# Wider stationary operand in the split value products of a transformer block

## The chip, the cores and the metric

The kernel is one program on one core of one Trainium2 chip. The metric is the device time of one execution in microseconds; the time before is the median of three executions. The profile is of one further execution, with its own time.

## The reference, cut to what matters

The kernel computes a conditioned transformer block on `x` of 2 x 2048 x 576 (16 heads of 36, a hidden layer of 2304):

```
q, k, v = split(modulate(rmsnorm(x)) @ qkv_w.T + qkv_b)      # q, k normed per head
attn = softmax(q @ k.T)                                      # per row of the batch and head
o = attn @ v                                                 # <- the change is in this product
x = x + gate_msa * (o @ proj_w.T + proj_b)
x = x + gate_mlp * (gelu(modulate(rmsnorm(x)) @ fc1_w.T + fc1_b) @ fc2_w.T + fc2_b)
```

All is float32. Where the kernel multiplies in the type fp32r, it splits operands into a high and a low part and adds the products of the parts.

## The kernel before

There are two phases. The first (`qkv_phase`, lines 115 to 630) computes q, k and v and writes them to scratch tensors in HBM. The second (`main_phase`, lines 649 to 1500) has an attention stage and then a stage of projection and MLP. In the trace the attention stage lies between about 480 and 1960 us.

The attention stage runs over 64 units `u`. A unit is one pair of heads, one row of the batch and one block of 512 queries. In a unit there are 16 blocks `kt` of 128 keys. For each one TensorE computes the scores of both heads transposed (`score`, line 1361: two products, each with 110 rows and 128 columns of stationary `kT` and 512 moving columns of `qT`), ScalarE takes the exponential of both heads at once (line 1017), and TensorE multiplies the exponentials with v.

This last product has two forms. For the eight key blocks 4 to 11 (`WHOLE`) it is `value` (lines 1372 and 1373): plain float32, with a stationary of 64 columns for one head and of 37 for the other. For the other eight (`SPLITS`) it is `split_value` (line 1386), which the change touches. VectorE has split the exponentials into `p_hi` (line 1187) and `p_lo` (line 1193). For each of the two heads TensorE multiplies `p_hi` and then `p_lo`, 128 x 512 each, by the same stationary `vx`. That makes 4 products for one key block, 32 in a unit, 2048 in the kernel.

`vx[r]` is a tile of 128 x 8 x 2 x 128: for each split key block and each head it has 128 columns. For head 0 these are 64 columns of the high part of v and then 64 of its low part; for head 1 it is the low part first. In each 64, the first 36 are v and the next is the column of ones that gives the sum of the exponentials. `split_v` (lines 1170 to 1180) writes all 128 of them, and the columns behind the 37th of a half come from a scratch tensor that was filled with ones. Before the change a product uses the first `VW` = 64 + 36 + 1 = 101 columns and writes rows 0 to 100 of a PSUM bank, `OA` for head 0 and `OBK` for head 1. Those who read the banks, `take_oa` on VectorE (line 1140) and `take_ob` on ScalarE (line 1023), read rows 0 to 100.

The order of TensorE's work is written out by hand (lines 1452 to 1476). A unit starts with three scores, then alternates the four split products of a key block with the two score products of another, has another run of three scores in the middle and one near the end, and ends with the eight `value` pairs. Split products of a unit's last four key blocks run in the next unit. A split group waits once, for the `p_lo` of its key block (line 1383). The projection of the first block, `proj` (line 1404: 14 products with 128 columns), is fitted between the units from `LAST` = 60 on.

Of the kernel before, what the change touches and what calls it, by code (L numbers as in the profile page):

```python
# [22 lines left out]
BLK = 512  # L23
# [12 lines left out]
VW = 64 + HD + 1  # L36
# [8 lines left out]
def wait(eng, sem, value):  # L45

    if isinstance(value, int) and value <= 0:
        return
    eng.wait_ge(sem, value)
# [599 lines left out]
def main_phase(nc, ctx, ps, qk_hi, qk_lo, v_s, m_s, l_s, oh_s, ol_s, xT, w2, wp, w1, outT, ident, ones, unbounded, mod, gate_b,  # L649
# [12 lines left out]
    def at(name, shape, dt, offset):  # L662
        return nc.alloc_sbuf_tensor_at(name, shape, dt, offset=offset)
# [18 lines left out]
    vx = [at(f"vx{j}", [P, NS, 2, VP], F32R, VX + j * 8 * NS * VP) for j in range(B)]  # L682
# [160 lines left out]
    with nc.Block() as block:  # L843
# [497 lines left out]
        def _(pe):  # L1341
# [33 lines left out]
            def split_value(u, j):  # L1375

                r, q = u // C % B, NS * u + j
                if u % C == 0 and j == 0:
                    pe.wait_ge(v_split, 4 * (u // C + 1))
                if j == 0:  # L1380
                    wait(pe, oa_evac, u)
                    wait(pe, ob_evac, u)
                pe.wait_ge(plo_done, q + 1)
                for h, out in enumerate((OA, OBK)):
                    for n, part in enumerate((p_hi[:, q % HIGHS], p_lo[:, j])):
                        mm = pe.matmul(out[0:VW], vx[r][:, j, h, 0:VW], part[:, h * BLK:(h + 1) * BLK],  # L1386
                                       start=j == 0 and n == 0, stop=j == NS - 1 and n == 1)
                mm.then_inc(rv_mm, 1)

# [62 lines left out]
            for u in range(NU):  # L1452
                for kt in range(3):
                    score(u, kt)
                for j in range(EARLY):
                    if u > 0:
                        split_value(u - 1, EARLY + j)
                    if j < 3:
                        score(u, 3 + j)
                if u in (LAST + 1, LAST + 2):  # L1460
                    proj(0, 2 * (u - LAST) - 1)
                for kt in range(6, 9):
                    score(u, kt)
                for j in range(3):
                    split_value(u, j)
                    score(u, 9 + j)
                if LAST <= u < LAST + 3:
                    if u == LAST:
                        pe.wait_ge(wplo_done, KC)
                    proj(0, 2 * (u - LAST))  # L1470
                for kt in range(12, 15):
                    score(u, kt)
                split_value(u, 3)
                score(u, 15)
                for kt in WHOLE:
                    value(u, kt)
# [75 lines left out]
```

## Time and profile before

| | us |
|---|---|
| median of 3 executions | 3021.05 |
| lowest, highest | 3019.34, 3022.63 |
| the profiled execution | 3016.58 |
| its span, first to last instruction | 3014.8 |

The granted TensorE clock over the span is 0.99 of full speed. TensorE (PE) is busy for 97% of the span, VectorE (DVE) for 66%, ScalarE (ACT) for 53%, GpSimd (POOL) for 7%. Busy times of matmuls overlap, since a matmul's record reaches into the next one: so a product's price on TensorE is read from the distance between the starts of two products, or from a piece of the chain of waits divided by its count, and not from its mean duration. PEld is the loading of stationary operands, which lies beside the matmuls.

### The profile page before, as it was taken

The page shows a single profiled execution, that of the slowest core. Times are in us where ns is not written, and L with a number is a line of the kernel's source. Part 1 is how long each engine was busy: PE and PEld are TensorE (multiplying, and loading weights), DVE is VectorE, ACT ScalarE, POOL GpSimd, SP SyncE. Part 2 cuts the span into 40 slices and gives each one's busy share as a digit, 9 for nine tenths or more (in the row PEclk, how much of TensorE's full clock was granted, in tenths as well). Part 3 has the DMA queues.
Part 4 walks back from the last instruction along what each step waited for, and adds up shares of the span by engine and source line. Part 5 has one row for each costly group of instructions (what it writes and reads, how often), then busy time and mean ns, then how long its engine had stood idle before and what let it go on. Part 6 is the DMA issues. An engine that isn't in the chain of part 4 may idle for free.

```text
span 3014.8 us, 35206 instructions
## 1 busy us (share of the span) xinstructions
PE 2920.2 (97%) x12968; PEld 2134.4 (71%) x12968; DVE 2003.6 (66%) x2687; ACT 1593.7 (53%) x1926; POOL 220.3 (7%) x153
## 2 busy tenths in 40 slices
PE   8999996999999999999999999999999999999998
PEld 7898994566566566566565566678888888888886
DVE  5887775888888888888888888744243342424332
ACT  3333324677677677677677676634343443434342
POOL 3232301000000000000000000080000000000000
PEclk9999997999999999999999999999999999999999
DMA  5464545122222222222222223242222222322121
GB/s 209 145 191 157 173 137 157 58 84 74 71 85 75 60 82 75 71 85 74 63 79 75 73 83 96 75 163 66 93 88 71 83 75 75 96 94 88 40 70 44
DMA packets 238406, 282.84 MB, mean 94 GB/s; under 512 B 34912, under 2 KB 143968, under 8 KB 237344
## 3 DMA queue, kind: packets, MB, share of 16 engines
q1 hardware_dynamic: 232992, 270.18, 28.9%
q10 hardware_dynamic: 5248, 10.49, 1.0%
q8 instruction: 99, 1.62, 0.2%
q14 instruction: 67, 0.55, 0.1%
HBM read 195.66 MB, written 84.67 MB: 93 GB/s over the span
## 4 chain that ended last, share of the span: by engine, by line
PE 78%; ACT 3%; DVE 2%; DMA 1%; SPq 0%; issue 0%; POOL 0%; DVEq 0%; POOLq 0%
PE ps L1386 16%; PE ps L1361 15%; PE ps L1445 14%; PE ps L1428 14%; PE ps L1373 13%; PE ps L1404 4%; ACT prob L1017 2%; PE ps L1372 2%; ACT gated L1070 1%; DVE x L1244 0%; DMA x<-xT 0%; DMA lt<-osb 0%; DVE w_lo L1238 0%; SPq L861 0%; DVE x L1248 0%
## 5 line engine op out<-in xcount | busy, mean ns | idle before, releaser
L1017 ACT ACTIVATE p_r<-ps 128x1024 f32<-128x1024 f32 x512 | 482.5, 1033 | 405.0 <-PE ps L1361 405.0
L1361 PE MATMUL ps<-qT,kT 110*128 110x512 f32 x2048 | 594.9, 402 | 34.1 <-DMA qT<-m_scratch 19.7
L1193 DVE TENSOR_TENSOR p_lo<-p_r,p_hi 128x1024 fp32r<-128x1024 f32 x512 | 612.8, 1217 | 0.0
L1017 ACT ACTIVATE prob<-ps 128x1024 f32<-128x1024 f32 x512 | 498.1, 1032 | 48.2 <-PE ps L1361 47.9
L1361 PEld LDWEIGHTS ps<-qT,kT 110*128 110x128 f32 x2048 | 376.8, 189 | 205.0 <-issue 51.6
L1187 DVE CAST p_hi<-p_r 128x1024 fp32r<-128x1024 f32 x512 | 353.9, 695 | 164.4 <-ACT p_r L1017 161.6
L1372 PE MATMUL ps<-prob,vp 128*64 128x512 f32 x1024 | 453.2, 595 | 0.0
L1373 PE MATMUL ps<-prob,vp 128*37 128x512 f32 x1024 | 451.8, 594 | 0.0
L1316 DVE TENSOR_TENSOR a_lo<-act,a_hi 128x512 fp32r<-128x512 f32 x144 | 102.0, 709 | 523.0 <-ACT a_hi L1060 523.0
L1445 PE MATMUL ps<-a_hi,w 128*128 128x512 f32 x1296 | 416.7, 394 | 2.9 <-DVE a_lo L1316 2.9
L1386 PE MATMUL ps<-p_hi,vx 128*101 128x512 f32 x1024 | 406.0, 397 | 0.0
L1386 PE MATMUL ps<-p_lo,vx 128*101 128x512 f32 x1024 | 403.9, 394 | 0.0
L1058 ACT ACTIVATE act<-ps,f1b_t 128x512 f32<-128x512 f32 x144 | 99.2, 689 | 511.4 <-PE ps L1428 511.4
L1373 PEld LDWEIGHTS ps<-prob,vp 128*37 128x37 f32 x1024 | 111.5, 114 | 248.3 <-issue 248.3
L1428 PE MATMUL ps<-mh_hi,w_hi 128*128 128x512 f32 x720 | 282.9, 393 | 4.1 <-DVE w_lo L1238 4.1
L1445 PEld LDWEIGHTS ps<-a_hi,w 128*128 128x128 f32 x1296 | 244.1, 188 | 56.1 <-DVE a_lo L1316 3.3
L1445 PE MATMUL ps<-a_lo,w 128*128 128x512 f32 x720 | 281.2, 391 | 0.0
L1428 PE MATMUL ps<-mh_hi,w_lo 128*128 128x512 f32 x720 | 280.5, 390 | 0.0
L1428 PE MATMUL ps<-mh_lo,w_hi 128*128 128x512 f32 x576 | 225.3, 391 | 0.0
L1386 PEld LDWEIGHTS ps<-p_lo,vx 128*101 128x101 f32 x1024 | 171.1, 167 | 68.9
L1386 PEld LDWEIGHTS ps<-p_hi,vx 128*101 128x101 f32 x1024 | 169.0, 165 | 57.6 <-issue 1.5
L593 PE MATMUL ps<-w_hi,h_hi 128*128 128x432 f32 x640 | 182.5, 366 | 9.6 <-DVE h_hi L70 8.2
(163 smaller groups left out, 3617.7 us busy)
## 6 DMA issues: line engine op xcount, KB each, us to landing
w_raw<-w SPq DMA_DIRECT2D x144, 320.0 KB, 2.9
qk_hi_scratch<-aw SPq DMA_DIRECT2D x32, 576.0 KB, 3.1
qk_lo_scratch<-aw SPq DMA_DIRECT2D x32, 576.0 KB, 4.4
kT<-qk_hi_scratch SPq DMA_DIRECT2D x128, 144.0 KB
qT<-qk_hi_scratch SPq DMA_DIRECT2D x128, 144.0 KB
v_scratch<-stv SPq DMA_DIRECT2D x32, 512.0 KB, 2.7
vp<-v_scratch SPq DMA_DIRECT2D x16, 1024.0 KB, 9.4
xb<-xT SPq DMA_DIRECT2D x8, 1280.0 KB, 10.1
```

The source lines that it names most:

```text
L593: mm = pe.matmul(ps[:, q, 0:PIECE], a[:, r, k, cols], w[:, k, q * PIECE:(q + 1) * PIECE], start=k == 0 and n == 0, stop=k == KF and n == 1)
L1017: act.activation(out, ps[:, 2 * slot:2 * slot + 2, :].rearrange("p a b -> p (a b)"), ACT.Exp).then_inc(exp_done, 1)
L1187: dve.tensor_copy(p_hi[:, q % HIGHS], p_r[:, j]).then_inc(phi_done, 1)
L1193: dve.tensor_tensor(p_lo[:, j], p_r[:, j], f32(p_hi[:, q % HIGHS]), ALU.subtract).then_inc(plo_done, 1)
L1316: dve.tensor_tensor(a_lo[:, slot], act32[:, slot], f32(a_hi[:, slot]), ALU.subtract).then_inc(alo_done, 1)
L1361: mm = pe.matmul(ps[:, 2 * (entry % RING) + h, :], kT[r][:, h, kt * P:(kt + 1) * P], qT[:, u % 2, h], start=True, stop=True)
L1372: pe.matmul(OA[0:64], vp[r][:, kt, 0:64], prob[:, j, 0:BLK], start=False, stop=False)
L1373: pe.matmul(OBK[64:VW], vp[r][:, kt, 64:VW], prob[:, j, BLK:2 * BLK], start=False, stop=False).then_inc(fv_mm, 1)
L1386: mm = pe.matmul(out[0:VW], vx[r][:, j, h, 0:VW], part[:, h * BLK:(h + 1) * BLK], start=j == 0 and n == 0, stop=j == NS - 1 and n == 1)
L1404: mm = pe.matmul(proj_bank(i, m), w[:, k, m * P:(m + 1) * P], a[:, k], start=k == 0 and n == 0, stop=k == KF and n == 1)
L1428: mm = pe.matmul(ps[:, 5 + slot, :], w[:, slot, c], a[:, i % 2, c], start=c == 0 and n == 0, stop=c == KF and n == 1)
L1445: mm = pe.matmul(ps[:, m, :], w, a[:, slot], start=k == 0 and n == 0, stop=k == FC - 1 and n == len(parts) - 1)
```

## The change

In `split_value` the product takes all 128 columns of `vx` for the key block and head, and writes all 128 rows of the bank. Nothing else differs.

```diff
                 for h, out in enumerate((OA, OBK)):
                     for n, part in enumerate((p_hi[:, q % HIGHS], p_lo[:, j])):
-                        mm = pe.matmul(out[0:VW], vx[r][:, j, h, 0:VW], part[:, h * BLK:(h + 1) * BLK],
+                        mm = pe.matmul(out, vx[r][:, j, h], part[:, h * BLK:(h + 1) * BLK],
                                        start=j == 0 and n == 0, stop=j == NS - 1 and n == 1)
                 mm.then_inc(rv_mm, 1)
```

## Rows read from the trace of the kernel before

**Rows 1.** The page: busy us, share of the span and instructions of each engine.
```profile
PE 2920.2 (97%) x12968; PEld 2134.4 (71%) x12968; DVE 2003.6 (66%) x2687; ACT 1593.7 (53%) x1926; POOL 220.3 (7%) x153
```

**Rows 2.** The page: chain that ended last, share of the span by line.
```profile
PE ps L1386 16%; PE ps L1361 15%; PE ps L1445 14%; PE ps L1428 14%; PE ps L1373 13%; PE ps L1404 4%; ACT prob L1017 2%; PE ps L1372 2%; ACT gated L1070 1%; DVE x L1244 0%; DMA x<-xT 0%; DMA lt<-osb 0%; DVE w_lo L1238 0%; SPq L861 0%; DVE x L1248 0%
```

**Rows 3.** Windows: us, busy us and count by engine, clock, DMA share, GB/s.
```profile
1400.00:1600.00 200.00, 198.12 (x853) 119.28 (x852) 172.13 (x231) 137.53 (x151) 0.00 (x0) 1.00 0.26 74
2400.00:2600.00 200.00, 199.82 (x875) 163.99 (x874) 70.25 (x98) 80.51 (x121) 0.00 (x0) 1.00 0.25 80
```

**Rows 4.** Chain in order of time, attention stage: start us, us, what, count.
```profile
1494.87 0.48 PE ps L1361 x2
...
1508.62 0.93 PE ps L1386 x4
1509.55 0.46 PE ps L1361 x2
1510.01 0.93 PE ps L1386 x4
1510.94 0.47 PE ps L1361 x2
1511.40 0.93 PE ps L1386 x4
1512.33 1.37 PE ps L1361 x6
```

**Rows 5.** Groups by form: busy us, mean ns of one, idle before.
```profile
L1386 PE MATMUL ps<-p_hi,vx 128*101 128x512 f32 x1024 | 406.0, 397 | 0.0
...
L1386 PEld LDWEIGHTS ps<-p_lo,vx 128*101 128x101 f32 x1024 | 171.1, 167 | 68.9
L1386 PEld LDWEIGHTS ps<-p_hi,vx 128*101 128x101 f32 x1024 | 169.0, 165 | 57.6 <-issue 1.5 <-DVE oa L1140 0.6
...
L1404 PEld LDWEIGHTS ps<-o_hi,wp_lo 128*128 128x128 f32 x200 | 37.6, 188 | 8.0
```

**Rows 6.** Timeline of PE from 1508.4: start us, us, instruction.
```profile
1508.46 0.40 PE L1386 MATMUL ps<-p_hi,vx 128*101 128x512 f32 x1
1508.69 0.40 PE L1386 MATMUL ps<-p_lo,vx 128*101 128x512 f32 x1
```

**Rows 7.** Timeline of PEld from 1507.5.
```profile
1508.46 0.17 PEld L1386 LDWEIGHTS ps<-p_lo,vx 128*101 128x101 f32 x1
1508.69 0.16 PEld L1386 LDWEIGHTS ps<-p_hi,vx 128*101 128x101 f32 x1
```

**Rows 8.** Chain in order of time: projection products from 1855 and from 1874.
```profile
1856.14 3.21 PE ps L1404 x14
...
1876.11 3.17 PE ps L1404 x14
```

**Rows 9.** Chain in order of time, MLP stage, from 2600.
```profile
2600.89 3.19 PE ps L1428 x14
```

**Rows 10.** Waits of VectorE: us in total, times, longest.
```profile
DVE oa L1140 <- PE ps L1386: 30.4, 59, 0.5
```

**Rows 11.** Waits of weight loads: us in total, times, longest.
```profile
PEld ps L1361 <- ACT prob L1017: 39.4, 64, 0.6
...
PEld ps L1386 <- issue: 1.5, 5, 0.4
...
PEld ps L1386 <- DVE oa L1140: 0.6, 2, 0.3
```

## The prediction

> **What bounds the kernel now.** I read the page's busy times first. TensorE is busy for 97% of the span and VectorE, the next, for 66% [rows 1]. The chain that ended last says where it counts: the split products of line 1386 are its largest single line, 16% of the span, and the scores of line 1361 have 15% [rows 2]. Then the windows, since the share of the whole span mixes stages: in the 200 us from 1400, in the attention stage, TensorE has work for 198.12 us, VectorE for 172.13 and ScalarE for 137.53 [rows 3]. So in the stage of the change TensorE sets the pace, and VectorE, which splits the exponentials, has 14% to spare. A nanosecond more or less on each split product arrives in the time nearly whole, 2048 times.
>
> What a split product costs now can't be read from its mean duration of 397 ns [rows 5], because the records overlap. In the timeline two of them start 0.23 us apart [rows 6]. The chain has the better number, pieces of 0.93 us for four: 0.93 / 4 = 232.5 ns each [rows 4]. Check: 2048 x 232.5 ns = 476 us, and 16% of 3014.8 us is 482 us [rows 2]. It holds.
>
> **The change part by part.** There is one edit, and it has four effects to price.
>
> *The stationary load.* It reads 128 columns where it read 101. The loads at line 1386 take 165 and 167 ns on average, and a load of 128 columns at line 1404 takes 188 [rows 5]: 22 ns more. Is that on the path? The load of the next product starts with the running product, at 1508.46 both, takes 0.17 us, and the next product starts at 1508.69 [rows 6, 7]. So 232.5 - 166 = some 66 ns lie between the end of a load and the start of its product. With 188 ns there remain 44. The running product's stream hides the load, and 22 of the 66 ns of cover are used up. If the cover were gone altogether, the price would be 22 ns x 2048 = 45 us. The rows of 128 columns say it is not gone: with the 188 ns load, products start 227 to 229 ns apart (next paragraph).
>
> *The distance between two products.* The moving operand is 512 columns before and after, so the stream of a product is the same. What the trace doesn't show is a split product with 128 columns, so I bound its distance by products that have them. Below: the projection in the middle of the attention stage, beside the same work of VectorE and ScalarE, 3.17 / 14 = 226.4 ns, and 3.21 / 14 = 229.3 at another place [rows 8]; the first MLP product 3.19 / 14 = 227.9 [rows 9]. Above: the scores between the split groups, which also load 128 columns (but 110 rows), 0.46 / 2 = 230 to 0.47 / 2 = 235, and once 0.48 / 2 = 240 ns [rows 4]; six scores in a row take 1.37 / 6 = 228.3. So the bounds per split product are 226.4 - 232.5 = -6.1 ns and 240 - 232.5 = +7.5 ns, which is -12.5 us and +15.4 us over 2048.
>
> I choose 230.5 ns, 2 ns less than now, or -4.1 us. The reason: long runs of one form with 128 columns go at 226 to 229 wherever they are, and no run with 101 columns does; but the scores right beside the split products have 128 columns and don't go faster than these, which says that most of the excess comes from alternating between forms, operands and banks, and that stays. The score rows are the nearest in place and pattern, so I stay nearer to them.
>
> At this place a rule can be weighed. By the Trainium skill, page "TensorE: Matmul & The Clock Gate", section "Back-to-back issue gap", the distance of products at full clock follows from the moving columns alone. With it the sum would be zero, since 512 stays 512. The trace agrees in part: the distance hardly depends on the stationary's width, but rows of one moving width range from 226.4 to 240 ns [rows 4, 8], above the page's 216, so something else adds 10 to 24 ns, and that is where this change could act.
>
> *Exposed loads.* Where the load comes after a wait, its whole length counts. At line 1386 that is so 5 + 2 times, with 1.5 and 0.6 us in total [rows 11]: 7 x 22 ns = 0.2 us, nothing. If each of the 512 split groups had its first load exposed it would be 11 us; the rows say they don't, since VectorE's parts are ready before. The 64 waits of a score's load for ScalarE (39.4 us, [rows 11]) are in the scores, and their length is set by the exponential of an earlier score; they neither shrink nor grow.
>
> *Rows 101 to 127 of the banks.* They are written and read by nobody. `take_oa` waits for the last split product (59 times, 30.4 us, [rows 10]) and reads 101 rows as before. VectorE's split of v already covers 128 columns, and no transfer changes. Cost 0; a cost would have to be in writing more rows of PSUM, and the projection's 128 rows at 226.4 ns [rows 8] show none. Nor is anything late next if the products come closer: even 12.5 us over the 64 units is 0.2 us in a unit of some 22.5, against the 14% that VectorE has free.
>
> Sum: -4.1 us + 0.2 us = -3.9 us. The profiled execution took 3016.58 us, 4.5 us less than the median of 3021.05 and 1.8 us more than its span. As nothing in the change touches what lies around the span, I put the difference on the median: 3017.1 us.
>
> **The rivals.**
>
> *The partial width is what costs.* Then all split products fall to the distance of the projection's. For it: no piece of line 1386 is under 0.93 us for four, while each long run of full-width products beside it is faster [rows 4, 8]. Against it: the scores between the split groups are full-width and at 230 to 235 ns [rows 4], and the projection at 1856 has 229.3. Time: 3021.05 - 12.5 = 3008.6 us. A rule of the skill (same page, section "Weight-path perf modes") would point this way: a fast weight load is on with exactly 128 weights of a type that is not FP32. The trace speaks against its being at work here, 188 ns for the 128-column load against 165 for 101 [rows 5], and a load that is hidden gains nothing by being faster; by it the sum would be at most this rival's.
>
> *The longer load costs* (the other side). Mechanism: the stationary for the next product is read while the moving operand streams, and has to be in place some time before the swap. The cover falls from 66 to 44 ns. If the swap needs more than 44 ns, or if the longer reading holds up the stream, each split product gets later, as the scores may be showing with 235 to 240 ns in the places where they alternate. It decides as soon as the distance passes 232.5 + 3 = 235.5 ns. At 237.5, the middle of 235 and 240, it is +5 x 2048 ns = +10.2 us: 3031.3 us. Against it: the 188 ns load under a distance of 226.4 ns [rows 5, 8] leaves only 38 ns and costs nothing.
>
> *The clock.* More columns at work could bring the granted clock down. The MLP stage, full width throughout and TensorE busy for 199.82 of 200 us, has 1.00 [rows 3], so I give it no more than a part of the slower case.
>
> **How the numbers follow.** What a measurement of this kernel can tell from no change is about 0.2%, 6 us, or 3 ns per split product. The forecast (230.5 ns, with values from 229.5 to 235.5) has 0.50 and is within it. The rival of the partial width, with gains of 3 to 6 ns, has 0.36, and the slower one 0.14. The range reaches down to 3007, the faster rival with 1.6 us of scatter (half of that of the three runs), and up to 3027, where +6 us is the end of the within case; beyond it lies most of the slower case and little of the others.
>
> **What the profile of the changed kernel would show.** The loads at line 1386 in the form 128*128 with a mean of 188 ns. The pieces of line 1386 in the chain: 0.92 for four if I am right, 0.91 or less for the first rival, 0.95 or more for the slower one. VectorE's and ScalarE's busy times and the clock of 1.00 unchanged. The scores' pieces unchanged; if they too move, the distance belongs to the pair of neighbours and not to the product, and my count of 2048 is too small. The forecast is wrong if the line's share of the chain falls by more than 6 us or grows at all beyond that.

## The result, and the profile after

The changed kernel takes 3014.16 us (median of 15 executions) against 3020.88 us for the kernel before beside it (15 executions): ratio 0.9979, 95% interval 0.9971 to 0.9986. It is faster by some 6 us, 0.2%, and the interval lies clear of no change. The forecast was 3017.1 us.

The page of the changed kernel, busy times and then the chain by line, as in [rows 1, 2]:

```profile
PE 2912.2 (97%) x12968; PEld 2178.5 (72%) x12968; DVE 2002.6 (67%) x2687; ACT 1590.7 (53%) x1926; POOL 219.1 (7%) x153
...
PE ps L1386 16%; PE ps L1361 15%; PE ps L1445 15%; PE ps L1428 14%; PE ps L1373 13%; PE ps L1404 4%; ACT prob L1017 2%; PE ps L1372 2%; ACT gated L1070 1%; DVE x L1244 0%; DMA lt<-osb 0%; DMA w_raw<-w 0%; DVE w_lo L1238 0%; DMA kT<-qk_hi_scratch 0%; DVE x L1248 0%
```

Only PEld has grown, by 44 us: 2048 loads that are 22 ns longer. The windows of the same two stages [rows 3] show the same, and the clock at 1.00; the second window, where nothing was changed, is the control:

```profile
1400.00:1600.00 200.00, 198.33 (x856) 126.46 (x856) 172.48 (x232) 137.58 (x152) 0.00 (x0) 1.00 0.28 78
2400.00:2600.00 200.00, 199.82 (x875) 163.98 (x874) 74.02 (x103) 78.86 (x120) 0.00 (x0) 1.00 0.26 81
```

In 200 us of the attention stage TensorE now starts 856 matmuls instead of 853. The groups by form and the waits, as in [rows 5, 10]; the waits of a split load have hardly moved (7 times, 1.6 + 0.7 = 2.3 us, before 1.5 + 0.6 = 2.1):

```profile
L1386 PEld LDWEIGHTS ps<-p_lo,vx 128*128 128x128 f32 x1024 | 193.8, 189 | 43.9
L1386 PEld LDWEIGHTS ps<-p_hi,vx 128*128 128x128 f32 x1024 | 192.9, 188 | 45.7 <-issue 1.6 <-DVE oa L1140 0.7
...
DVE oa L1140 <- PE ps L1386: 28.4, 59, 0.5
```

**The length of a unit is the sharpest measure.** The six scores at the head of each of the 64 units are the only pieces of the chain `x6` that last about 1.6 us. Their starts are a unit apart. In the kernel before:

```profile
1415.40 1.61 PE ps L1361 x6
...
1528.15 1.61 PE ps L1361 x6
```

and in the changed one, with the pieces of one unit between them, as in [rows 4]:

```profile
1413.48 1.58 PE ps L1361 x6
...
1503.29 1.58 PE ps L1361 x6
1504.87 0.93 PE ps L1386 x4
1505.80 0.47 PE ps L1361 x2
1506.27 0.93 PE ps L1386 x4
1507.20 0.45 PE ps L1361 x2
1507.65 0.94 PE ps L1386 x4
1508.59 0.46 PE ps L1361 x2
1509.06 0.92 PE ps L1386 x4
1509.97 1.36 PE ps L1361 x6
...
1525.75 1.58 PE ps L1361 x6
```

Both stretches are five units: 112.75 / 5 = 22.550 us before, 112.27 / 5 = 22.454 after. The unit is 0.096 us shorter, and 64 x 0.096 = 6.1 us. That is an estimate from settled units: some of the first fourteen gain next to nothing, and in the two traces all units from the second on add up to 5.5 us. It accounts for the measured gain within its interval. In these two kernels nearly all units agree to 0.01 us, so a unit shows differences that the times alone leave open. The experiments below are read by it too; each has one profiled execution.

Where in the unit is it? The pieces of the split products hardly differ, 0.92 to 0.94 where they were 0.93 or 0.94; the score pieces are as much shorter: 1.58 for 1.61, 1.36 for 1.37, 0.45 and 0.46 for 0.46 and 0.47. The pieces end where modelled ends of matmuls lie, so starts are the better witness. Over all starts that follow the one before within 300 ns, the mean distance into a split product went from 233.1 to 231.5 ns, and into a score from 231.6 to 230.9. By where it stands: from a score into a split product 232.7 to 229.3, from `p_hi` to `p_lo` 233.6 to 231.7, from `p_lo` to `p_hi` 232.4 to 233.3 (means over every such pair of neighbours). So the gain is not an even one on each wide product. It is a shift of the pattern in which split products and scores follow one another.

### The profile page after: what moved, and what is told of

The parts are those of the page before. It is cut to its first block, busy times and chain, and to the rows that moved or that the text cites. A ratio compares the mean times of both kernels' runs of the same rounds, so it can differ in the third digit from the quotient of the medians.

```text
span 3009.5 us, 35206 instructions
## 1 busy us (share of the span) xinstructions
PE 2912.2 (97%) x12968; PEld 2178.5 (72%) x12968; DVE 2002.6 (67%) x2687; ACT 1590.7 (53%) x1926; POOL 219.1 (7%) x153
## 4 chain that ended last, share of the span: by engine, by line
PE 78%; ACT 3%; DVE 2%; DMA 1%; SPq 0%; issue 0%; POOL 0%; DVEq 0%; POOLq 0%
PE ps L1386 16%; PE ps L1361 15%; PE ps L1445 15%; PE ps L1428 14%; PE ps L1373 13%; PE ps L1404 4%; ACT prob L1017 2%; PE ps L1372 2%; ACT gated L1070 1%; DVE x L1244 0%; DMA lt<-osb 0%; DMA w_raw<-w 0%; DVE w_lo L1238 0%; DMA kT<-qk_hi_scratch 0%; DVE x L1248 0%
## 5 line engine op out<-in xcount | busy, mean ns | idle before, releaser
L1386 PE MATMUL ps<-p_hi,vx 128*128 128x512 f32 x1024 | 404.4, 395 | 0.1
L1386 PE MATMUL ps<-p_lo,vx 128*128 128x512 f32 x1024 | 404.1, 395 | 0.0
L1386 PEld LDWEIGHTS ps<-p_hi,vx 128*128 128x128 f32 x1024 | 192.9, 188 | 45.7 <-issue 1.6
L1386 PEld LDWEIGHTS ps<-p_lo,vx 128*128 128x128 f32 x1024 | 193.8, 189 | 43.9
```

The source lines that it names most:

```text
L1386: mm = pe.matmul(out, vx[r][:, j, h], part[:, h * BLK:(h + 1) * BLK], start=j == 0 and n == 0, stop=j == NS - 1 and n == 1)
```

## The experiments

Every kernel has the reference's arithmetic unless said. "Unit" is the length as above, over nine units from about 1415 us, where the kernel before has 22.550 us and the changed one 22.456.

**A series of products by itself, and the width in steps.** Four kernels. The first appends to the kernel before nine series of 48 products that nobody reads, one source line each. The core of it:

```diff
+            for q in range(48):
+                w, a = operands(q, VW)
+                pe.matmul(ps[0:VW, 7, :], w, a, start=True, stop=True)
```

> The kernel before with nine series of 48 products each behind its last product, when nothing else but the last output transfer is under way: fp32r, 512 moving columns, high and low parts in turn. In order: 128 columns into one bank twice, 101 columns, 64 columns, 128 and 101 in turn, 128 with a change of bank after every two, 101 with the same change, then groups of four with 128 columns and two with 110 rows by 128 columns, and groups of four with 101 columns and two with 110 rows by 128 columns. Width theory (a partial stationary costs by itself): 101 columns 231 to 233 ns from start to start, 128 columns 226.5. Mixture theory (a change of width between neighbours costs): 101 columns alone 226.5 as 128 columns, but 128 and 101 in turn 231 or more, and the last series 3 ns or more above the one before it. Nothing-in-isolation theory (the excess over 226.5 comes from waits and other engines in the attention stage): all series 226 to 228 ns.

The chain in order of time, one piece for each series in the order given:

```profile
3009.84 12.81 PE ps L1510 x48
3022.65 10.89 PE ps L1513 x48
3033.54 11.20 PE ps L1516 x48
3044.74 11.04 PE ps L1519 x48
3055.78 11.35 PE ps L1523 x48
3067.13 10.94 PE ps L1526 x48
3078.07 11.21 PE ps L1529 x48
3089.28 11.17 PE ps L1533 x48
3100.45 11.16 PE ps L1537 x48
```

Divide by 48. The first piece is longer because its products begin at the lower clock (shown at the third series below). With 128 columns (line 1513) a product starts 226.9 ns after the one before, 226.8 by the starts themselves; with 101 (line 1516) it is 233.3, with 64 (line 1519) 230.0. 101 and 128 in turn (line 1523): 236.5. So the partial width costs 6.5 ns by itself, with nothing beside it. The change of bank (lines 1526, 1529) costs nothing: 227.9 with some ten products of settling at its head, and 233.5. And the last two series are groups of four and two as in the kernel, the two with 110 rows: they take 232.7 ns with 128 columns in the groups of four (line 1533) and 232.5 with 101 (line 1537). In a series, the advantage of the full width is gone beside products of another height.

The other three set the width in the kernel itself:

```diff
-                        mm = pe.matmul(out, vx[r][:, j, h], part[:, h * BLK:(h + 1) * BLK],
+                        mm = pe.matmul(out[0:112], vx[r][:, j, h, 0:112], part[:, h * BLK:(h + 1) * BLK],
```

> Split products with 112 columns. Width theory: a gain of 11/27 of the measured one of 6 us, so 2 to 3 us under the kernel before, ratio 0.999. Mixture theory: 112 is as unlike the scores' 128 as 101 is, so no gain, ratio 1.000. Rows-in-groups theory (what counts is only which of the four groups of 32 columns are full): the fourth group is partly used as with 101, ratio 1.000.

Measured: ratio 0.9995 (0.9986 to 1.0004), unit 22.54 us. By the unit, 0.01 us of the 0.095 is gained, where a slope with the width would give 0.04; the interval of the times doesn't exclude the 2 to 3 us. Here the starts show what a distance belongs to: the mean into a split product fell from 233.1 to 231.9 ns, and the mean into a score rose from 231.6 to 233.0.

> Split products with 127 columns. Width theory: nearly the whole gain, ratio 0.998, and a unit of the attention stage of 22.46 us as with 128. Mixture theory and the theory of full groups: only 128 is equal and full, so no gain, ratio 1.000 and a unit of 22.55 us as with 101.

Measured: 0.9985 (0.9976 to 0.9994), unit 22.46 us. Nearly all of the gain, so neither "exactly 128" nor "equal to the neighbour" is the condition. The mixture theory falls in its simple form. The gain sits in the neighbours: into a split product the mean is 233.0 ns as before the change, into a score it is 229.0 instead of 231.6.

The third gives only the products with `p_hi` the full width:

```diff
+                        mm = pe.matmul(out[0:(P, VW)[n]], vx[r][:, j, h, 0:(P, VW)[n]], part[:, h * BLK:(h + 1) * BLK],
```

> 128 columns for the products with p_hi, 101 for those with p_lo; rows 101 to 127, which nobody reads, get the high part only. Width theory: half the gain, 3 us, ratio 0.999. Mixture theory: width now changes at every product, so slower than before by up to the 2 to 6 ns of a changed neighbour times 2048, 4 to 12 us, ratio 1.001 to 1.004.

Measured: 1.0001 (0.9992 to 1.001), unit 22.57 us, 0.02 longer than before the change. By the unit, half the products wide is a little worse than none: in turn, the two widths disturb each other, as the 236.5 ns of the series say. The times alone can't tell it from no change.

**The scores' rows.** If the scores' 110 rows are what hides the gain, giving them 128 must bring it out. Rows 110 to 127 are ones in `kT` and zeros in `qT`, so the scores keep their values:

```diff
-    kT[0] = following("kT0", [PKW, 2, N], F32R)
+    kT[0] = following("kT0", [P, 2, N], F32R)
...
-    qT = following("qT", [PKW, 2, 2, BLK], F32R)
+    qT = following("qT", [P, 2, 2, BLK], F32R)
...
+            pool.memset(f32(qT[96:P]), 0.0).then_inc(kones, 1)
+            pool.wait_ge(kones, 1)
             for r in range(B):
-                pool.memset(f32(kT[r][96:PKW]), 1.0).then_inc(kones, 1)
+                pool.memset(f32(kT[r][96:P]), 1.0).then_inc(kones, 1)
...
```

> The changed kernel, and the scores too take all 128 rows: the stationary kT and the moving qT get rows 110 to 127 (ones times zeros), so that score and split products have one form, 128 x 128. Neighbour theory (the excess over 226.7 ns, the distance in isolation at full width, comes from the scores' 110 rows beside the split products' 128): both fall to 226.7 nearly everywhere in the attention stage, the 32 split products of a unit by some 5 ns and the 20 or more scores among them by 4 to 6, so a unit goes from 22.46 to about 22.2 us and the kernel is 15 to 20 us faster than the kernel before the change in addition to the 6 of the change, ratio 0.991 to 0.994. Rival (waits and the two engines beside it make the excess): no further gain, ratio 0.998.

> The kernel before, 101 columns in the split products, with the scores' 128 rows as in the run beside it. Theory that the width costs 6.6 ns by itself and the mixture with 110 rows hides it: here the split products stay at 233 ns, and the distance to the run with 128 columns is the full price of the width, 32 x 6.6 = 0.21 us a unit, 13.5 us over the kernel. Rival (width and rows only matter as a mixture): a gain here that is as large as with 128 columns, or none at all.

Measured: with 128 columns 0.9983 (0.9974 to 0.9992) and a unit of 22.42 us; with 101 columns 0.9998 (0.9989 to 1.0007) and 22.52 us. My expectation of another 15 to 20 us was wrong. The rows are worth 0.03 to 0.04 us a unit and the width 0.10 instead of the 0.21 expected, and the two add up: 22.55, 22.52, 22.46, 22.42. So the scores' height is not what hides the gain in the kernel: with it out of the way the width is worth 0.100 us a unit, and with it 0.095. The mean distance into a split product is 230.8 ns with all products 128 x 128, not the 226.7 of the series. So something else keeps them apart, and it is not the form of scores and split products.

**More widths alone.** Again series of 48 behind the kernel before, all from one line:

```diff
+            for q in range(48):
+                product(q, 112, 128)
```

> The kernel before with series of 48 products behind its last one, a bank change after every two: 64 of 128 columns to settle, then 96, 104, 112, 120 and 127 columns with 128 rows, then 110 rows with 128 columns, 110 rows with 101 columns, then groups of four with 128 rows and two with 110, groups of four with 128 and two with 96 rows, all with 128 columns, and 128 x 128 again. Width theory with a slope: distances fall evenly from 233.3 ns at 101 columns to 226.7 at 128, so 230.6 at 112 and 226.9 at 127. Theory of full groups of 32 columns: 96 columns 226.7, all of 104 to 127 at 233. Row theory: 110 rows alone is 226.7 as in the long runs of scores, and in groups with 128 rows 232.7; with 96 rows likewise if any change of row count costs, 226.7 if only a partly filled group of 32 rows does.

The timeline of PE, the first product of each form:

```profile
3026.23 0.39 PE L1506 MATMUL ps<-a_hi,w_hi 128*96 128x512 f32 x1
...
3037.27 0.39 PE L1506 MATMUL ps<-a_hi,w_hi 128*104 128x512 f32 x1
...
3048.26 0.40 PE L1506 MATMUL ps<-a_hi,w_hi 128*112 128x512 f32 x1
...
3059.46 0.40 PE L1506 MATMUL ps<-a_hi,w_hi 128*120 128x512 f32 x1
...
3070.65 0.39 PE L1506 MATMUL ps<-a_hi,w_hi 128*127 128x512 f32 x1
...
3081.53 0.40 PE L1506 MATMUL ps<-a_hi,w_hi 110*128 110x512 f32 x1
```

Start to start over 48: 96 columns 230.0 ns, 104 columns 229.0, 112 columns 233.3, 120 columns 233.1, 127 columns 226.7, and 101 columns with 110 rows 233.5. Neither a slope nor a step at a multiple of 32: both theories of the width fall. The longest loads, 127 and 128 columns, have the shortest distance. 110 rows throughout are as quick as 128 once settled (226.8 from the 13th on), and the groups of four and two give 232.8 with 110 and with 96 rows in the two: in a series the change of height costs, not the height.

**Waits and raises of semaphores.** In the attention stage every group has a wait and raises a semaphore; the series so far had none.

```diff
+            for q in range(72):
+                wait(pe, gate_done, KC * NB if q % 6 in (0, 4) else 0)
+                ...
+                if q % 6 in (3, 5):
+                    mm.then_inc(series_mm, 1)
```

> The kernel before with ten series of 72 products behind its last one, a bank change after every two. In order, with groups of four and of two as in the attention stage: 128 x 128 to settle; 128 x 128; the same with a satisfied wait ahead of each group; with a semaphore raised behind each group instead; with both; both, and the groups of two with 110 rows (as the changed kernel); both, 110 rows in the groups of two and 101 columns in the groups of four (as the kernel before); both, 101 columns throughout; 101 columns in the groups of four and 128 rows throughout, without wait and raise; 128 x 128 again. Theory of waits and raises: plain 128 x 128 at 226.7 ns, with waits or raises 230 or more, so that a group pattern at 128 never settles, and the four-and-two patterns with 128 and with 101 columns lie within 2 ns of each other, as in the kernel. Rival (other engines' traffic disturbs the attention stage): waits and raises change nothing, 226.7 at 128 and 233.3 at 101 columns.

```profile
3011.80 19.08 PE ps L1507 x72
3030.89 16.32 PE ps L1511 x72
3047.21 16.32 PE ps L1516 x72
3063.53 16.32 PE ps L1520 x72
3079.85 16.32 PE ps L1527 x72
3096.17 16.74 PE ps L1534 x72
3112.91 16.75 PE ps L1541 x72
3129.65 16.80 PE ps L1548 x72
3146.45 16.86 PE ps L1554 x72
3163.31 16.35 PE ps L1558 x72
```

16.32 / 72 = 226.7 ns without, with waits, with raises and with both: satisfied waits and raises cost TensorE nothing. The theory falls cleanly. Line 1534 is the changed kernel's pattern and line 1541 that of the kernel before: 232.5 and 232.6, alike again. 101 columns throughout (line 1548) give 16.80 / 72 = 233.3. Line 1554 has groups of four with 101 columns and of two with 128, as the kernel before, but 128 rows throughout: 16.86 / 72 = 234.2. Without a change of height the full width is worth 7.5 ns in this pattern, and with it nothing.

The first series also shows the clock. TensorE had stood still for the last gate until 3011.8 us, its products then start 426 to 427 ns apart, and the granted clock of the stretch from 3012 to 3017 us is 0.50, the lower of its two levels; from 3023 to 3100 us it is 1.00.

> Split products with 104 columns, which went at 229.0 ns alone, between the 233.3 of 101 and 112 columns and the 226.7 of 127 and 128. If the distance alone carries over to the kernel in the measured proportion (101 to 128 columns: 6.6 ns alone, 0.094 us a unit), a unit comes down by 4.3/6.6 of that, from 22.55 to 22.49 us, ratio 0.9985 to 0.999. If only a full or nearly full array gains, or if each width has its own pattern in the mixture, the unit stays at 22.54 as with 112 columns or goes anywhere between 22.4 and 22.6.

Measured: 1.0007 (0.9998 to 1.0016), unit 22.56 us. 104 columns are quicker alone than 101 by 4.3 ns and no quicker in the kernel; the units alternate between 22.54 and 22.58 us there. So a distance measured alone doesn't carry over in proportion.

**Where operands and results lie.** The last series, all with 128 columns but one. Each is appended as a whole; the diff sets the plain series against the one that mattered, which takes the stationary of the groups of four from the tile `w2c`:

```diff
-                pe.matmul(ps[:, 6 + q // 2 % 2, :], (w1_hi, w1_lo)[q % 2][:, q // 4 % 2, q % KC],
+                pe.matmul(ps[:, 6 + q // 2 % 2, :], (w2c[:, q // 2 % FC, 0:P] if q % 6 < 4 else w1_hi[:, q % 2, q % KC]),
```

> The kernel before with ten series of 72 products behind its last one, 128 x 128 unless said. In order: to settle; the plain form (a bank change after every two, each product overwrites); products that accumulate into the two banks; groups of two in other banks than groups of four; one stationary for two products in a row, with the moving operand changing at each, as in the split products; stationary operands from two distant tiles for groups of four and of two; moving operands likewise; all of these together; all together with 101 columns in the groups of four; the plain form again. Operand theory (the excess over 226.7 ns that is left in the attention stage with all products 128 x 128 comes from where the operands and results lie or from accumulating): one of the single changes and the combination go at 229 or more. Rival (it comes from outside TensorE: VectorE, ScalarE and transfers): every series with 128 columns 226.7 ns, the one with 101 columns in its groups of four 233 to 235.

```profile
3031.09 16.32 PE ps L1508 x72
3047.41 16.32 PE ps L1511 x72
3063.73 16.32 PE ps L1514 x72
3080.05 16.32 PE ps L1517 x72
3096.37 16.56 PE ps L1520 x72
3112.93 16.32 PE ps L1523 x72
3129.25 16.57 PE ps L1526 x72
3145.82 16.63 PE ps L1530 x72
3162.45 16.32 PE ps L1533 x72
```

Accumulating (line 1511), other banks (1514), one stationary twice (1517), distant moving operands (1523): all 226.7 ns. The groups of four from `w2c` (1520): 230.0. All together (1526): 230.1, and with 101 columns in the groups of four (1530) 231.0. The plain form again (1533): 226.7. The 230.1 is close to the 230.8 ns that the attention stage keeps with everything 128 x 128. So most of that rest can come from where the stationary operands lie, with no other engine at work.

It is not that there are two tiles: the plain series takes its stationary in turn from `w1_hi` and `w1_lo`, two tiles as well, at 226.7 ns. Nor does it need a mixture. In the kernel itself the second MLP product (line 1445) is 128 x 128 throughout and takes every stationary from `w2c`, and its longest run in the kernel before is

```profile
2996.60 6.43 PE ps L1445 x28
```

6.43 / 28 = 229.6 ns, or 228.9 from start to start, with 229, 232 and 226 ns in turn to its end. So a long run of one full form isn't always at 226.7 either. What it is about `w2c` (its place, or the steps in which it is read) was not tried, nor was the attention stage run with its tiles placed otherwise.

**The value products of the whole keys, and all three together.**

```diff
-                pe.matmul(OBK[64:VW], vp[r][:, kt, 64:VW], prob[:, j, BLK:2 * BLK], start=False, stop=False).then_inc(fv_mm, 1)
+                pe.matmul(OBK[64:P], vp[r][:, kt, 64:P], prob[:, j, BLK:2 * BLK], start=False, stop=False).then_inc(fv_mm, 1)
```

> The changed kernel, and the whole-key value products of the second head use 64 columns and write rows 64 to 127, where 37 columns and rows 64 to 100 were used. If a partly filled group of columns costs there too, a pair falls from 429 ns by up to 7 ns, eight pairs in a unit: up to 0.05 us of 22.46 and 3 us over the kernel, ratio 0.997 against the kernel before. Rival (in plain float32 the pair is bound by its four passes over the moving operand): pairs stay at 429 ns, ratio 0.998.

Measured: 0.9985 (0.9976 to 0.9994), unit 22.47 us against 22.46 for the change alone: nothing gained. A pair starts 429 ns after the last one in both.

> All three widenings together: split products with 128 columns, scores with 128 rows, whole-key value products with 64 columns for both heads. The unit was 22.55 us before, 22.46 with the split products alone, 22.42 with the scores' rows too. If the effects add, it is 22.42 or, where the value products gain as well, down to 22.37 us, ratio 0.9965 to 0.998. Rival: the effects are patterns of one mixture and don't add, anything between 22.4 and 22.5.

Measured: 0.998 (0.997 to 0.9989), unit 22.42 us, as with the scores' rows alone. No version here is measurably better than the changed kernel: by the unit the scores' rows are worth 64 x 0.039 = 2.5 us more, which the times don't resolve.

## Why the prediction was right, point by point

**Right: TensorE's spacing is the price.** The gain is the change of a unit, 64 times, and VectorE and ScalarE have the same work as before (2002.6 and 1590.7 us busy, before 2003.6 and 1593.7).

**Right: the longer load is hidden.** The loads take 188 and 189 ns, as forecast, and the exposed ones are 7 as before with 2.3 us. The slower rival, a load that runs into the swap, is refuted beyond this kernel: alone, the widths with the longest loads are the quickest (226.7 ns with 127 and 128 columns).

**Right in direction, and the size was off: -2 ns x 2048 = -4.1 us.** Measured are 6.1 us by the unit. Over the same nine units the mean into a split product went from 232.9 to 231.5 ns, 32 x 1.4 ns = 0.044 us a unit, which is 2.8 us in the kernel: a size near the term, and less than half of the gain. The rest is what the prediction had left out and named as a sign: the neighbours moved too. The 28 scores that follow within 300 ns start 0.8 ns sooner, 0.022 us; the wait for ScalarE near the end of a unit, 597 to 582 ns from start to start, gives 0.014; the step from the last score to the value products, 327 to 318, gives 0.009; and the first step of a unit, 341 to 335, gives 0.006. 0.044 + 0.022 + 0.014 + 0.009 + 0.006 = 0.095 us. The count of 2048 was too small, because a distance belongs to a pair of products.

**In part luck.** By the prediction's own split, a gain of 3 ns per split product, or 6 us, is where its forecast ends and the faster rival begins, and 6.1 us by the unit stands on that border. Its term for the split products was a choice between rows, not a mechanism, and the neighbours' share that brought the total there was at zero. Its other sign did not come: the pieces of line 1386 were to be 0.92 us and are 0.92 to 0.94, on average 0.93 as before, since they end at modelled ends. And it gave a measurement a grain of 6 us; with 15 executions of each kernel the interval is 0.15% wide, and the change stands clear of it.

**The rival of the partial width was right alone and wrong in the kernel.** Its 6.1 ns from the projection's rows are 6.6 in the series. 32 x 6.6 ns would be 0.21 us a unit, 13.5 us. The kernel shows 0.095, less than half. Why the rest doesn't arrive is argued from the series and not shown in the kernel. Two things made the price of the width shrink there: a change of height between products (232.5 to 232.8 ns with 101 as with 128 columns), and a stationary from `w2c` (230.1 ns with 128 columns in the groups of four, 231.0 with 101). The first is not what does it in the kernel, where scores of 128 rows left the width's worth at 0.100 us a unit. The second was tried in a series alone.

The prediction had said that most of the excess comes from alternating between forms, operands and banks. In the series, alternating heights or widths and the place of the stationary are shown to do it; banks, moving operands, accumulating and semaphores are shown not to. In the kernel, one form for scores and split products took the mean into a split product from 231.5 to 230.8 ns, and what keeps the other 4 ns above 226.7 is open. It had also read from its rows that the distance hardly depends on the stationary's width; alone it does, by 6.6 ns, and the rows of the kernel before did not show it.

**The rule of the moving columns.** By the Trainium skill, page "TensorE: Matmul & The Clock Gate", section "Back-to-back issue gap", the formula for the distance at full clock has the moving columns alone, 216 ns for 512, and by it the change would be worth zero. The section calls that the gap of an isolated product and gives about 131 ns for a stream of products with loads, set by both operations; no run here shows either figure. The runs disagree with the formula: with 512 moving columns throughout and the granted clock at 1.00, the stationary's width alone moves the distance between 226.7 and 233.3 ns.

**What stays open** is why 96 to 120 columns lie between 229 and 233.3 ns and 127 and 128 at 226.7. The pattern is neither even nor at steps of 32. No mechanism is shown. Open as well is what in the attention stage lets less than half of the 6.6 ns arrive.

## What to carry to other kernels

Where TensorE sets the pace with back-to-back products, a partial stationary may cost 3% of each (6.6 of 233 ns), even though fewer columns are loaded: if the extra columns hold finite data and the extra rows are read by nobody, take the full width. Expect the whole of it at most in long runs of one form. Where products of different heights or widths alternate, or the stationary comes from another tile, measure in place: here less than half arrived, and half-wide mixtures were no better than none.

## What the runs showed of the hardware

- Settled distance of fp32r products with 512 moving columns, each with its own load, clock at its upper level: 226.7 ns with 127 or 128 columns, 233.3 with 101 or 112, 233.1 with 120, 230.0 with 96 or 64, 229.0 with 104. 110 rows with 128 columns: 226.8, with 101 columns 233.5.
- Mixtures: 101 and 128 columns in turn 236.5 ns; groups of four with 101 and two with 128 columns 234.2; any groups of four with 128 rows and two with 110 or 96, 232.5 to 232.8.
- At 128 x 128 with stationary operands from `w2c`: 230.0 ns where the groups of four have them, 228.9 in a run of 28 products that all have them, against 226.7 from `w1_hi` and `w1_lo`.
- After a change of form it takes up to some ten products until the distance is settled: the first eight of a series of 128 x 128 after mixed ones were 236, 224, 231, 236, 228, 233, 230 and 227 ns apart.
- A satisfied wait ahead of each group and a raise behind it cost TensorE nothing: 16.32 us for 72 products in all four cases.
- A pair of float32 value products takes 429 ns with 37 or with 64 columns in its second half.
